# Gated FFN with low-rank experts on one core: two pieces of wi taken to another queue and place, the first piece laid out in two blocks, the common record loaded and split earlier

## The reference

```python
x = hidden_states                                    # [8, 256, 256]
hidden_i = jnp.einsum('bsd,fd->bsf', x, wi)          # wi [1024, 256]
hidden_i += ALPHA * jnp.einsum('bsr,fr->bsf', jnp.einsum('bsd,rd->bsr', x, common_wi_a), common_wi_b)
hidden_i += _expert_lora(x, expert_ids, experts_wi_a, experts_wi_b)
hidden_i = jax.nn.relu(hidden_i)
hidden_o = jnp.einsum('bsf,df->bsd', hidden_i, wo)   # wo [256, 1024]
hidden_o += ALPHA * jnp.einsum('bsr,dr->bsd', jnp.einsum('bsf,rf->bsr', hidden_i, common_wo_a), common_wo_b)
hidden_o += _expert_lora(hidden_i, expert_ids, experts_wo_a, experts_wo_b)
return x + hidden_o
```

## Time and profile before

| | |
|---|---|
| median of 3 timed executions | 120.17 us (119.84 to 120.77) |
| profiled execution, its own time | 120.01 us |
| its span, first to last instruction | 118.2 us |
| PE busy | 113.1 us, 96% of the span |
| DVE, ACT, POOL busy | 60.3, 47.4, 42.0 us |
| granted TensorE clock | 1.000 |

### The profile page before, as it was taken

One profiled execution on the slowest core, in us unless ns is written; L12 is line 12 of the kernel. 1 busy time (PEld: TensorE's weight loads), 2 busy tenths in 40 slices (PEclk: granted clock), 3 DMA queues, 4 the chain that ended last, 5 costly groups with the idle time before them and its releaser, 6 DMA issues.

```text
span 118.2 us, 1984 instructions
## 1 busy us (share of the span) xinstructions
PE 113.1 (96%) x730; PEld 103.7 (88%) x730; DVE 60.3 (51%) x104; ACT 47.4 (40%) x94; POOL 42.0 (36%) x60
## 2 busy tenths in 40 slices
PE   6979998989999999999999999999999999999990
PEld 6758887878889999988889999988889999999990
DVE  4486999999964421134444335134444135525121
ACT  4467589343973511323663523213343113332100
POOL 2024699989899020225573006616000020000000
DMA  3999799998980035106000015006000010111121
GB/s 97 372 358 361 222 367 370 333 310 287 246 309 7 6 64 205 44 3 222 0 6 0 0 48 176 30 20 188 33 0 0 0 38 11 44 44 44 44 94 44
DMA packets 8748, 14.93 MB, mean 126 GB/s; under 512 B 1042, under 2 KB 5138, under 8 KB 8738
## 3 DMA queue, kind: packets, MB, share of 16 engines
q1 hardware_dynamic: 8018, 13.49, 34.9%
q10 hardware_dynamic: 720, 1.31, 3.2%
HBM read 12.70 MB, written 2.10 MB: 125 GB/s over the span
## 4 chain that ended last, share of the span: by engine, by line
PE 77%; DVE 11%; DMA 5%; SPq 3%; issue 1%; ACT 1%
PE bank_o L732 36%; PE bank_h L627 24%; PE bank_o L728 5%; DMA b_raw<-in_rec_b 5%; PE bank_h L661 5%; DVE hid L475 4%; DVE common_st L475 2%; PE bank_low L678 2%; PE bank_o L751 1%; DVE xT L480 1%; DVE low_stack L475 1%; PE bank_o L627 1%; PE bank_low L627 1%; DVE b_stack L491 1%; PE bank_h L704 1%
## 5 line engine op out<-in xcount | busy, mean ns | idle before, releaser
L732 PE MATMUL bank_o<-wcat,hid 128*128 128x272 f32 x336 | 45.1, 289 | 0.0
L732 PEld LDWEIGHTS bank_o<-wcat,hid 128*128 128x128 f32 x336 | 43.4, 188 | 0.0
L627 PE MATMUL bank_h<-xT,wiT 128*128 128x512 f32 x156 | 39.8, 395 | 0.6 <-DVE wiT L562 0.6
L627 PEld LDWEIGHTS bank_h<-xT,wiT 128*128 128x128 f32 x156 | 27.7, 189 | 6.4 <-issue 1.2
L475 DVE SCALAR_TENSOR_TENSOR hid<-bank_h,hid 128x512 fp32r<-128x512 f32 x26 | 17.3, 687 | 13.4 <-ACT hid L379 13.4
L379 ACT ACTIVATE hid<-bank_h 128x512 fp32r<-128x512 f32 x26 | 14.9, 598 | 17.1 <-PE bank_h L661 16.9
L552 DVE TENSOR_TENSOR o_sb<-bank_o,x_nat 128x256 f32<-128x256 f32 x16 | 6.7, 423 | 19.5 <-PE bank_o L751 17.4
L276 POOL TENSOR_TENSOR b_stack<-b_raw,b_stack 32x1024 fp32r<-32x1024 f32 x6 | 14.4, 2406 | 3.5 <-ACT b_stack L367 3.4
L267 POOL CAST a_stack<-a_raw 128x192 fp32r<-128x192 f32 x8 | 4.5, 560 | 18.1 <-DMA a_raw<-in_rec_a 18.1
L661 PEld LDWEIGHTS bank_h<-low_stack,b_stack 128*128 128x128 f32 x52 | 8.7, 189 | 2.0 <-DVE low_stack L475 0.6
L402 ACT ACTIVATE rank_sb<-bank_o 128x64 fp32r<-128x64 f32 x14 | 3.1, 223 | 18.0 <-PE bank_o L732 18.0
(11 more groups left out here) (58 smaller groups left out, 107.5 us busy)
## 6 DMA issues: line engine op xcount, KB each, us to landing
b_raw<-in_rec_b SPq DMA_DIRECT2D x8, 512.0 KB, 5.6
x_nat<-in_x_n SPq DMA_DIRECT2D x4, 512.0 KB, 3.9
out<-o_sb SPq DMA_DIRECT2D x16, 128.0 KB, 1.7
x_raw<-in_x_t SPq DMA_DIRECT2D x6, 256.0 KB, 4.0
w_raw<-in_wo_t SPq DMA_DIRECT2D x4, 256.0 KB, 5.2
w_raw<-in_wi_t ACTq DMA_DIRECT2D x3, 256.0 KB, 4.9
a_raw<-in_rec_a SPq DMA_DIRECT2D x8, 96.0 KB, 3.8
bo_raw<-in_rec_bo SPq DMA_DIRECT2D x8, 96.0 KB, 3.6
```

The lines of the kernel that those rows point to most:

```text
L627: nc.tensor.matmul(up_bank(q, m)[:, :], wiT_at(sw, k, m), xT[q % 2][sx][:, k, :], start=start, stop=False)
L732: last = nc.tensor.matmul(bank_o[g % NO][:, 0:WIN], hid[q % 2][sh][:, m, tok], wcat[sw][:, m, win], start=(m == 0 and i == 0), stop=(m == ...
```

## The change

- SP's two loads of wi's piece 0 read two blocks of 128 KB that lie unbroken in HBM, where they read every second kilobyte of one of 256 KB. The shapes in SBUF are the same.
- ACT issues piece 1 of wi alone. Pieces 2 and 3 are issued by SP, right behind B of step 0.
- SP issues the common record next, ahead of x and A of step 1, where it came behind them.
- ACT and DVE split piece 1 of wi, then B of step 0, then piece 2, then the ranks, then piece 3. Before, all three pieces came ahead of B.
- DVE splits its part of the common record ahead of x of step 1, and POOL its part ahead of A of step 1.

```diff
             for k in range(KD):
-                sp.dma_start(w_raw[:, 0, k * 2 * P:(k + 1) * 2 * P], wi_t[0][:, k * 2 * P:(k + 1) * 2 * P]).then_inc(wi0_in[k], 16)
+                sp.dma_start(w_raw[:, 0, k * 2 * P:(k + 1) * 2 * P], wi_0[k]).then_inc(wi0_in[k], 16)
...
             load_b(0)
+            for i in range(2, PIECES):
+                sp.dma_start(w_raw[:, i, :], wi_t[i - 1]).then_inc(wi_in[i], 16)
+            sp.wait_ge(common_zero, 1)
+            for i in range(3):
+                sp.dma_start(common_raw[i * BLK:i * BLK + R, :], common).then_inc(common_in, 16)
             load_x(1)
             for n in range(PAIR):
                 expert.append(sp.value_load(idt[0:1, PAIR + n:PAIR + n + 1], min_val=0, max_val=E - 1))
                 load_a(1, n)
-            sp.wait_ge(common_zero, 1)
-            for i in range(3):
-                sp.dma_start(common_raw[i * BLK:i * BLK + R, :], common).then_inc(common_in, 16)
             load_b(1)
...
             split_a(0)
             pool.wait_ge(a_ready, PAIR)
+            split_common()
+            pool.wait_ge(common_a_lo, 1)
             split_a(1)
             pool.wait_ge(a_ready, 2 * PAIR)
-            split_common()
-            pool.wait_ge(common_a_lo, 1)
...
-            for i in range(1, PIECES):
-                act.dma_start(w_raw[:, i, :], wi_t[i]).then_inc(wi_in[i], 16)
+            act.dma_start(w_raw[:, 1, :], wi_t[0]).then_inc(wi_in[1], 16)
...
-                for i in range(1, PIECES):
-                    split_wi_hi(i)
+                split_wi_hi(1)
                 split_b_hi(0, 0)
                 split_b_hi(0, 1)
+                split_wi_hi(2)
                 ranks_in_hi(0)
+                split_wi_hi(3)
...
-                for i in range(1, PIECES):
-                    split_wi_lo(i)
+                split_wi_lo(1)
                 split_b_lo(0, 0)
                 split_b_lo(0, 1)
+                split_wi_lo(2)
                 ranks_in_lo(0)
+                split_wi_lo(3)
+                common_b()
                 for k in range(KD):
                     split_x_lo(1, k)
-                common_b()
```

More of the change, by code:

```diff
@@ L15, with conditional_ffn @@
 STAGES = [("up", 0), ("up", 1), ("down", 0), ("up", 2), ("down", 1), ("up", 3), ("down", 2), ("down", 3)]
-def conditional_ffn(nc, x_t, x_n, ids, wi_t, wo_t, rec_a, rec_b, rec_bo, rec_ao, common, out):
+def conditional_ffn(nc, x_t, x_n, ids, wi_0, wi_t, wo_t, rec_a, rec_b, rec_bo, rec_ao, common, out):
     P = 128
@@ L22, in conditional_ffn @@
     D = KD * P
-    PIECES = wi_t.shape[0]
+    PIECES = wo_t.shape[0]
     PIECE = wi_t.shape[2]
@@ L846 @@
     wi_t = given["wi"].reshape(MF // 2, 2 * P, KD, P).transpose(0, 3, 2, 1).reshape(MF // 2, P, KD * 2 * P)
+    wi_0, wi_t = wi_t[0].reshape(P, KD, 2 * P).transpose(1, 0, 2), wi_t[1:]
     wo_t = given["wo"].reshape(D, MF // 2, 2, P).transpose(1, 3, 2, 0).reshape(MF // 2, P, 2 * D)
@@ L861 @@
     common = np.concatenate([given["common_wo_a"], given["common_wo_b"].T], axis=1)
-    laid = dict(x_t=x_t, x_n=x_n, ids=ids, wi_t=wi_t, wo_t=wo_t, rec_a=rec_a, rec_b=rec_b, rec_bo=rec_bo, rec_ao=rec_ao, common=common)
+    laid = dict(x_t=x_t, x_n=x_n, ids=ids, wi_0=wi_0, wi_t=wi_t, wo_t=wo_t, rec_a=rec_a, rec_b=rec_b, rec_bo=rec_bo, rec_ao=rec_ao, common=common)
     nc = bacc.Bacc("TRN2", target_bir_lowering=False, num_devices=1)
```

## The result

The changed kernel takes 120.87 us (median of 20 executions) and the kernel before 120.17 (20): a ratio of 1.0084, 95% interval 1.0057 to 1.0111. It is slower, by 0.7 us of the medians. The profiled execution took 120.75 us, its span is 119.0 (before: 120.01 and 118.2), so the profile has the loss.

A forecast was written before the change was run, and what follows sets the result against it. DVE's handover of the ranks of step 1 (T) was taken as the bound; -1.22 (B earlier), +1.44 (wi subtractions), -0.32 (waits behind POOL) and +0.25 less small gaps made some 0.0: 120.0 us, 8-in-10 range 118.8 to 121.5.

The forecast's parts named there:

- T: The moment DVE hands the ranks of step 1 to PE, said to set the time: 24.55 before, 24.57 forecast.
- waits behind POOL: DVE's waiting for POOL's cast and subtraction of the common record: 2.58 us where it was 2.9, so -0.32.
- hold of 0.89: POOL's cast of the common record, from 11.45, was to keep DVE from piece 2's low part until 12.75.
- Loads: B of step 0 lands 3.6 after issue, at 8.25, 1.22 us gained; pieces 2 and 3 at 10.2 and 10.85.
- The record at 11.45: Landing of the common record, 240 KB at B's pace behind pieces 2 and 3; up to 12.3 if its loads are slower.
- Two subtractions of wi behind B: On DVE, the low parts of pieces 2 and 3 move behind B of step 0, adding 1.44 us.
- Held by POOL: DVE's subtractions of wi and POOL's long operations block one another; piece 3's low part waits until 15.86 for POOL's subtraction.
- not held: Rival: POOL does not hold DVE's subtractions, PE sets T at 23.56, 1.0 us less, 119.0; chance 0.20.
- POOL gets ahead of piece 2: Rival: the common record lands early, POOL's operations precede piece 2's low part, PE stands still; 2.0 more, 122.0; chance 0.08.
- B does not come earlier: Rival: the load of B of step 0 gains nothing, the 1.22 is missing, 121.2; chance 0.12.
- PE's new wait: PE needs piece 2's low part at 12.82 and gets it at 13.47, a wait of 0.65 us, with DVE still setting T.
- Piece 0 in two blocks at 0: The new layout of wi's piece 0 gives nothing on the path, because DVE's 0.91 idle ahead of B takes it up.

The follow-up runs named there:

- after_wide_common: The changed kernel with the common record as one load of 96 partitions with zero rows instead of three of 16: 121.05 us, 1.0059 of the kernel before.
- splits_only: The kernel before with all its loads as they were, only the splits of wi's pieces 2 and 3 moved behind B: ratio 1.0158 to the kernel before.
- two_blocks: The kernel before with only wi's piece 0 laid out as two unbroken blocks: 120.69 us, 1.0034 of the kernel before.
- splits_off_pool: The kernel before with wi's splits moved behind B, loads unmoved, and the common record's cast on ACT and subtraction on DVE: 120.11 us, 0.9989 of the kernel before.
- off_pool_again: The kernel before with only POOL's work on the common record moved (cast to ACT, subtraction to DVE), a repeat run: 119.40 us, 0.9928 of the kernel before.
- after_off_pool: The changed kernel with the common record's cast on ACT and its subtraction on DVE, behind x of step 1: 119.79 us, 0.9956 of the kernel before.
- wi_off_pool: The kernel before with wi's loads and splits moved as in the change and the common record's splits taken off POOL: 120.19 us, 0.9984 of the kernel before.
- after_record_first: The changed kernel with the common record's three loads issued ahead of wi's pieces 2 and 3: 123.34 us, 1.0201 of the kernel before.
- after_piece2_on_act: The changed kernel with piece 2 of wi issued by ACT again, behind piece 1: 122.92 us, 1.0227 of the kernel before.

## Why the prediction was wrong

The bottleneck, T, was the right one: T moved 0.75 and the span 0.8. The forecast of T was 24.57, and 25.30 was measured: 0.73 later. Of this 0.61 is B's landing and 0.27 the waits behind POOL, less 0.06 for the two subtractions and 0.09 for gaps (the bullets below). Here are the ends of DVE's operations, forecast and by the chain shown above:

| | forecast | measured |
|---|---|---|
| B of step 0 | 11.86 | 12.43 |
| piece 2's low part | 13.47 | 13.15 |
| ranks | 14.17 | 13.87 |
| piece 3's low part | 16.58 | 15.24 |
| common record, DVE's part | 17.29 | 18.18 |
| x of step 1 | 18.72 | 19.66 |
| ranks of step 1 (T) | 24.57 | 25.30 |

That the second and third ends came out near the forecast is luck: B was 0.57 late, and the hold of 0.89 ahead of piece 2 did not come.

- **The failed step is "Loads"**, the times at which B, wi's pieces and the record land. B was to land 3.6 after its issue, at 8.25; it took 4.2 and landed at 8.85, so its term is -0.61, not -1.22 (DVE's B began at 9.96, before at 10.57). The price of 3.6 came from one other load of the same size, 8 us later. A slow stretch does not tell the two apart, since that load ran through one as well (183 and 119 GB/s from 12 to 14). Over its 3.65 us the queues moved 263 GB/s, over the 4.22 of this one 315: 0.96 and 1.33 MB. So this load took longer while more was moved beside it, and the forecast had "nothing ahead of it but piece 1 and A", without a price for what would run beside it. Between 8.15 and 9.06 lay B's first landing in every run whose wi pieces were moved as in the change and whose A stood ahead of B; the forecast was the good end of that. With the old order up to B the same landing lay between 9.25 and 10.57 (five profiles), so 0.61 is the gain between two single executions.
- **The record at 11.45, "up to 12.3"**: 13.53. The rate of B was used for it, and for the pieces ahead of it, though the profile of before showed transfers at 183 and 119 GB/s while the record was loaded. This table was not used. So POOL's subtraction ended at 17.51, not 15.86, and the term for waits behind POOL is 0.65 + 2.13 + 0.08 = 2.86, which is -0.05 against before, not -0.32. after_wide_common shows that B's landing alone would not have saved the forecast.
- **Two subtractions of wi behind B, +1.44**: 2 x 0.69 = 1.38, right. With gaps at +0.03, where the forecast had some +0.12 (0.25 less the old order's small gaps), the sum measured is -0.61 + 1.38 - 0.05 + 0.03 = +0.75.
- **Held by POOL**: right in kind, and the rival "not held" is out (piece 3 waited 0.65, the common record 2.2; with the record off POOL these waits were gone, with the subtraction cut most of them). The order was another one: POOL's cast came behind piece 2 and in front of piece 3, since the record was late.
- **"POOL gets ahead of piece 2"**, 122.0, did not come, by the same lateness. splits_only is its kin: DVE late by 1.1 us, and POOL ahead three times.
- **"B does not come earlier"**, 121.2, is nearest to what happened: half of the gain was missing.
- **PE's new wait**, 0.65 forecast, was 0.34 from start to start: PE needed piece 2's low part at 12.87, as thought (12.82), and DVE had it at 13.15 instead of 13.47.
- **Piece 0 in two blocks at 0**: its second half came at 4.95 instead of 6.21 and PE's wait of 0.6 for it went, but PE reached the ranks of step 0 at 11.00, as before at 10.95 (below). On the path 0 was right, and two_blocks shows no difference in time.

What is shown of the cause: in the profile, T's 0.75 is 1.38 of moved subtractions less 0.61 of B. By experiment, the splits behind B cost 0.6% with the record off POOL (splits_off_pool against off_pool_again) and 1.6% with it there (splits_only). That POOL's work on the record, taken away, brings the changed kernel below the kernel before is no proof, since the same edit gains 0.7% without the change. With the record off POOL the change costs 0.3% (after_off_pool), and wi's move 0.6% (wi_off_pool), over the kernel before with that edit; the intervals are as wide as these figures, so the split of the 0.8% between wi behind B and the waits is known only roughly. Not settled is why transfers are slow while the record is in flight, 16 or 96 partitions wide, and why they are at 5.5 to 6.5 us.

The Trainium skill ("SBUF — State Buffer", section "Who interferes with whom") says that whoever issues first gets the shared pair of ports for the whole instruction and the other blocks fully. The traces agree: x, the common record or a piece of wi waited, whichever DVE had next when POOL was in its 2.4 to 2.7 us. The prediction put both operations on the common record under a rule on two inputs. The first reads one tile alone (L507, common_st from common_raw), and it waited too: 2.49 beside POOL's subtraction, 0.41 with the record off POOL.

## What to carry to other kernels

Where two engines block each other, moving work on one of them does not cost its length: look which long operations of the other it will meet at its new time, and move the work off one engine if it can be done elsewhere for less than the wait (1.22 us on DVE and 1.05 on ACT for 2.9 of waiting here). Price a load by what that same load took and by what will be moved beside it, not by its bytes at the best rate. And follow every resource that reaches the joint (here POOL's chain, which ended 0.6 us before DVE's) before calling the gain or the loss of one of them the result.

## What the runs showed that was not expected

- **A halt of PE costs twice.** After PE's wait of 1.71 and, four matmuls later, of 0.26 in splits_off_pool, eight matmuls took 3.65 us (2.11 in the changed kernel). The table by stage there, with the granted clock third from the end:

```profile
13.00:14.00 1.00, 1.00 (x4) 0.55 (x4) 0.97 (x2) 1.00 (x3) 0.00 (x0) 1.00 0.86 135
14.00:15.00 1.00, 0.74 (x3) 0.57 (x3) 0.97 (x2) 0.87 (x2) 0.34 (x1) 0.64 1.02 237
15.00:16.00 1.00, 1.00 (x4) 0.81 (x3) 0.97 (x3) 0.00 (x0) 0.97 (x2) 0.50 0.94 266
...
17.00:18.00 1.00, 1.00 (x5) 0.79 (x4) 0.94 (x3) 0.20 (x1) 0.38 (x1) 0.66 0.99 377
```

  0.50 is the lower of the two levels, 1.2 GHz. It came only after PE had resumed and held for some 3.4 us (the shares of 0.64, 0.50, 0.50 and 0.66 from 14 to 18). after_record_first, with a wait of 2.95, shows the same (clock 0.50 at 16 to 18), splits_only too; after_piece2_on_act with waits of 1.1 and 1.0 does not.
- **Early matmuls at half pace under a full clock.** In the changed kernel PE's first six real matmuls start 0.43 to 0.56 us apart, the later ones 0.23, and all 24 together take 6.92 us from 4.24; the column of the granted clock says 1.00 from 4.2 to 8. Before, the first six took 1.70 at once. That is where the earlier half of piece 0 was lost; why they were slow is not shown.
- **Loads of one queue overlap.** Piece 3 of wi was issued ahead of the record's three loads (6.00 and 6.70 to 7.91). A third of the record's arrivals were in at 12.03, ahead of the last of piece 3 at 12.46. The three loads count on one semaphore, so it is not shown that one of them came whole before piece 3.
